# Routed experts: weights stationary with inner units on the partitions, unrolled over 71 tiles, weight-fold products spread over eight tiles

## What is computed

```
logits = x @ Wr / 16                       # 8 experts, top 2 of logits + rb
w      = softmax of the two chosen logits
h      = (x @ W1[e]) * silu(x @ W3[e])     # 256 -> 512
out    = sum of w_e * (h @ W2[e]) over the two chosen e   # 512 -> 256
out   += (x @ Ws1 * silu(x @ Ws3)) @ Ws2   # shared expert
```

## Time and profile before

| | us |
|---|---|
| median of 3 runs | 1294.36 (1294.14 to 1297.22) |
| profiled execution, whole | 1297.05 |
| its span | 1295.3 |
| TensorE busy | 1098.8 (85%) |
| VectorE, ScalarE, GpSimd busy | 843.1, 622.1, 685.3 |
| mean granted clock of TensorE | 0.954 |

### The profile page before, as it was taken

How to read it: one execution, slowest core, us unless ns; L and a number is a source line. 1 busy time by engine, 2 the same in 40 slices (tenths; PEclk the granted TensorE clock), 3 DMA queues, 4 the chain that set the end, 5 groups by cost and what they waited for, 6 DMA issues and landing times. The chain is left out here.

```text
span 1295.3 us, 27552 instructions
## 1 busy us (share of the span) xinstructions
PE 1098.8 (85%) x8532; PEld 829.3 (64%) x8533; DVE 843.1 (65%) x1791; ACT 622.1 (48%) x1483; POOL 685.3 (53%) x794
## 2 busy tenths in 40 slices
PE   4877877888647999799999999997498889699998
PEld 2555555555436787466666656654387777599997
DVE  3999899888747666444444444454588887566664
ACT  3666666666623555233233213322344444566664
POOL 7677677766306766499999566001656650100000
PEclk9999899999868999899999999998699999799999
DMA  1422222222154888735441101112334330111110
GB/s 33 127 91 99 76 100 89 85 85 94 62 191 162 285 274 269 225 136 185 155 154 57 57 25 57 57 53 69 107 115 120 121 106 33 50 50 50 49 49 34
DMA packets 113782, 137.19 MB, mean 106 GB/s; under 512 B 12368, under 2 KB 102448, under 8 KB 111920
## 3 DMA queue, kind: packets, MB, share of 16 engines
q1 hardware_dynamic: 104480, 101.63, 24.5%
q0 software_dynamic: 9232, 34.67, 7.8%
HBM read 83.83 MB, written 52.43 MB: 105 GB/s over the span
## 5 line engine op out<-in xcount | busy, mean ns | idle before, releaser
L253 POOL TENSOR_TENSOR bd<-T,hmask 128x1024 f32<-128x1024 f32 x64 | 150.5, 2372 | 6.9 <-ACT T L371 6.9
L360 ACT ACTIVATE pr<-S,nmx 128x128 f32<-128x128 f32 x512 | 139.3, 396 | 3.9 <-DVE nmx L284 3.9
L956 ACT CAST hT<-HT 128x512 f16<-128x512 f32 x72 | 42.1, 585 | 198.7 <-PE HT L914 198.7
L411 PE MATMUL S<-bd,T 128*128 128x512 f32 x256 | 126.4, 618 | 0.0
L893 PE MATMUL YB<-wm,hT 128*128 x864 | 106.5, 273 | 3.6 <-DVE hT L979 3.6
L893 PE MATMUL Ge<-wm,xT 128*128 x432 | 107.6, 386 | 1.0 <-DVE xT L984 1.0
L893 PE MATMUL Ue<-wm,xT 128*128 x432 | 105.7, 381 | 0.0
L893 PEld LDWEIGHTS YB<-wm,hT 128*128 128x128 f16 x864 | 84.4, 98 | 29.3 <-issue 4.5
L290 DVE SCALAR_TENSOR_TENSOR pT<-PT,pT 128x1024 f16<-128x1024 f32 x64 | 77.6, 1213 | 35.8 <-ACT pT L352 34.6
L1729 PE MATMUL H<-T6s,wm 128*128 128x256 f16 x768 | 96.5, 277 | 1.2 <-DVE T6s L1668 1.2
L1194 POOL DMA_INDIRECT yg<-ys_d,slot x64 | 66.0, 1032 | 58.3 <-POOLq L858 41.2
(11 more groups left out here) (248 smaller groups left out, 2571.1 us busy)
## 6 DMA issues: line engine op xcount, KB each, us to landing
stage<-in_L_ffn_W_dram SPq DMA_DIRECT2D x24, 512.0 KB, 6.1
xs_d<-zeros SPq DMA_DIRECT2D x36, 256.0 KB, 2.4
xe<-xs_d SPq DMA_DIRECT2D x72, 128.0 KB, 2.1
ys_d<-ye SPq DMA_DIRECT2D x72, 128.0 KB, 1.7
bw<-in_L_ffn_up_weights_dram POOLq DMA_DIRECT2D x7, 1024.0 KB, 5.8
bw<-_L_ffn_down_weights_dram POOLq DMA_DIRECT2D x7, 1024.0 KB, 5.6
xb<-in_x_dram SPq DMA_DIRECT2D x32, 128.0 KB, 2.1
cb<-in_ctx_dram SPq DMA_DIRECT2D x32, 128.0 KB, 2.2
```

What stands on the lines that cost most here:

```text
L253: nc.gpsimd.tensor_tensor(out=bd[:, a, c, :, :], in0=T0[:, a, C + c:C + c + 1, :].broadcast_to([P, HH, P]), in1=hmask[:, :, :], op=ALU.mul ...
L360: last = nc.scalar.activation(pr[:, h, i, :], S[h][:, i, :], ACT.Exp, bias=nmx[:, h, i:i + 1])
L411: last = nc.tensor.matmul(S[h][:, i:i + 4, :], T0[:, k % 2, h, :], bd[:, k % 2, h, i:i + 4, :], start=True, stop=True)
```

## The change

The routed stage is rewritten in four points.

- The first two products of an expert are turned round. A 128 by 128 slice of the weights is stationary and the 128 rows of `xT` move, so `Ge` and `Ue` come out with the expert's inner units on the partitions (four blocks `b` of 128 units, `hidden`). 24 products of 128 columns take the place of six of 512, and `hf4` is what `Ye` wants as its stationary side: the transposes of `he` and the bank `HT` are gone. ScalarE rounds `hf4` to the HI part, VectorE subtracts for the LO part, both now from SBUF. `Ye` is as before.
- The tiles are unrolled on all engines; there is no hardware loop in the stage.
- There are `NE` = 71 tiles, not 72.
- The fold's products come two a tile in tiles 48 to 55, into one bank of their own, the eight bias products in tile 47. VectorE copies them in the same tiles and takes the maximum of `wdn` at the end of tile 55, that of `wut` at the end of tile 64. GpSimd goes on after nine of the copies instead of all 17.

The core of the diff:

```diff
+    NE = (NB * TOPK * P + E * (P - 1)) // P
...
-            Ue = [ph.enter_context(nc.psum_tensor(f"Ue{i}", [P, H], F32)) for i in range(2)]
-            Ge = [ph.enter_context(nc.psum_tensor(f"Ge{i}", [P, H], F32)) for i in range(2)]
-            XB = ph.enter_context(nc.psum_tensor("XB", [P, 4, P], F32))
-            HT = ph.enter_context(nc.psum_tensor("HT", [P, HC, P], F32))
-            YB = [ph.enter_context(nc.psum_tensor(f"YB{i}", [P, 2, D], F32)) for i in range(2)]
-            XT, Ye = XB[:, 0:C, :], [y[:, 0, :] for y in YB]
-            Wf, Bf = [y[:, 1, :] for y in YB], XB[:, C, 0:FC]
+            Ue = [ph.enter_context(nc.psum_tensor(f"Ue{i}", [P, HC, P], F32)) for i in range(2)]
+            Ge = [ph.enter_context(nc.psum_tensor(f"Ge{i}", [P, HC, P], F32)) for i in range(2)]
+            XT = ph.enter_context(nc.psum_tensor("XT", [P, C, P], F32))
+            Ye = [ph.enter_context(nc.psum_tensor(f"Ye{i}", [P, D], F32)) for i in range(2)]
+            WB = ph.enter_context(nc.psum_tensor("WB", [P, 2, D], F32))
+            Wf, Bf = WB[:, 0, :], WB[:, 1, 0:FC]
...
-            LATE = 64
-            MID = 44
+            MID, LATE = 47, 64
...
-                    def product(bank, left, kind, e, chunks, width):
-
-                        for i, (xp, wp) in enumerate(PARTS):
-                            for c in range(chunks):
-                                last = nc.tensor.matmul(bank, left[:, xp, c, :],
-                                                        wm[:, kind, bass.ds(e, 1), wp, c * width:(c + 1) * width],
-                                                        start=i == 0 and c == 0, stop=i == 2 and c == chunks - 1)
+                    def hidden(bank, t, kind, e):
+
+                        for b in range(HC):
+                            for i, (wp, xp) in enumerate(PARTS):
+                                for c in range(C):
+                                    last = nc.tensor.matmul(
+                                        bank[:, b, :],
+                                        wm[:, kind, bass.ds(e, 1), wp, c * H + b * P:c * H + (b + 1) * P].rearrange(
+                                            "p o n -> p (o n)"),
+                                        xT[:, t % 2, xp, c, :], start=i == 0 and c == 0, stop=i == 2 and c == C - 1)
                         return last
 
-                    def body(t, k):
-                        if isinstance(t, int) and t < 0:
-                            if t == -1:
-                                xtr(0, 0)
-                            return
-                        a, b = k % 2, (k - 1) % 2
-                        before = experts.get(k - 1)
-                        if before is None and on4(t - 1):
-                            before = expert(t - 1)
-                        experts.clear()
-                        e = experts[k] = expert(t) if on4(t) else None
-                        if on4(t - 1):
-                            pe.wait_ge(s_he, t)
-                            if due(t - 1):
-                                pe.wait_ge(s_hTe, t - 1)
-                            for c in range(HC):
-                                last = nc.tensor.transpose(HT[:, c, :], he[:, b, c * P:(c + 1) * P], ident[:, :])
-                            last.then_inc(s_hT, 1)
-                        if on4(t):
+                    def fold(i):
+                        if i:
+                            pe.wait_ge(s_bv, i + i // FC)
+                        b, w = i % FC, (wut, wdn)[i // FC]
+                        nc.tensor.matmul(Wf, bdiag[:, i // FC, b * P:(b + 1) * P], w[:, b, 0:D],
+                                         start=True, stop=True).then_inc(s_bm, 1)
+
+                    transpose_rows(0)
+                    before = None
+                    for t in range(NE + 1):
+                        e = pe.value_load(tile_expert[0:1, t:t + 1], min_val=0, max_val=E - 1) if t < NE else None
+                        if t < NE:
                             pe.wait_ge(s_xte, t + 1)
-                            if due(t - 1):
+                            if t >= 2:
                                 pe.wait_ge(s_sl4, t - 1)
-                            product(Ge[a][:, :], xT[:, a, :, :, :], 0, e, C, H).then_inc(s_g, 1)
-                        xtr(t + 1, k + 1)
-                        if on4(t):
-                            if due(t - 1):
+                            hidden(Ge[t % 2], t, 0, e).then_inc(s_g, 1)
+                        if t == MID:
+                            pe.wait_ge(s_bo, FOLD_AT)
+                            for b in range(FC):
+                                nc.tensor.matmul(Bf[:, b:b + 1], bdiag[:, 0, b * P:(b + 1) * P], wut[:, b, D:D + 1],
+                                                 start=True, stop=True).then_inc(s_bm, 1)
+                        if MID < t <= MID + FC:
+                            fold(2 * (t - MID) - 2)
+                        transpose_rows(t + 1)
+                        if t < NE:
+                            if t >= 2:
                                 pe.wait_ge(s_he, t - 1)
-                            product(Ue[a][:, :], xT[:, a, :, :, :], 1, e, C, H).then_inc(s_u, 1)
-                        if on4(t - 1):
-                            pe.wait_ge(s_hTe, t)
-                            if due(t - 2):
+                            hidden(Ue[t % 2], t, 1, e).then_inc(s_u, 1)
+                        if MID < t <= MID + FC:
+                            fold(2 * (t - MID) - 1)
+                        if t >= 1:
+                            pe.wait_ge(s_hl4, t)
+                            if t >= 3:
                                 pe.wait_ge(s_yc, t - 2)
-                            product(Ye[b], hT[:, b, :, :, :], 2, before, HC, D).then_inc(s_ye, 1)
-
-                    steps(pe, RANGE4[0], MID, RANGE4[2], MID, 4, body)
-
-                    pe.wait_ge(s_bo, FOLD_AT)
-                    pe.wait_ge(s_xte, MID + 1)
-                    pe.wait_ge(s_yc, MID - 1)
-                    for b in range(FC):
-                        nc.tensor.matmul(Bf[:, b:b + 1], bdiag[:, 0, b * P:(b + 1) * P], wut[:, b, D:D + 1],
-                                         start=True, stop=True).then_inc(s_bm, 1)
-                    for i in range(2 * FC):
-                        b, w = i % FC, (wut, wdn)[i // FC]
-                        if i >= 2:
-                            pe.wait_ge(s_bv, i - 1)
-                        nc.tensor.matmul(Wf[i % 2], bdiag[:, i // FC, b * P:(b + 1) * P], w[:, b, 0:D],
-                                         start=True, stop=True).then_inc(s_bm, 1)
-                    pe.wait_ge(s_bv, 2 * FC + 1)
-                    steps(pe, MID, RANGE4[1], MID, RANGE4[3], 4, body)
+                            for i, (hp_, wp) in enumerate(PARTS):
+                                for b in range(HC):
+                                    last = nc.tensor.matmul(Ye[(t - 1) % 2][:, :], hh4[:, (t - 1) % 2, hp_, b, :],
+                                                            wm[:, 2, bass.ds(before, 1), wp, b * D:(b + 1) * D],
+                                                            start=i == 0 and b == 0, stop=i == 2 and b == HC - 1)
+                            last.then_inc(s_ye, 1)
...
+                        if t >= 0:
+                            act.wait_ge(s_he, t + 1)
+                            if t >= 2:
+                                act.wait_ge(s_ye, t - 1)
+                            nc.scalar.copy(hh4[:, t % 2, HI, :, :], hf4[:, t % 2, :, :]).then_inc(s_hh4, 1)
...
+                    def folded(i):
+                        b, w = i % FC, (wut, wdn)[i // FC]
+                        dve.wait_ge(s_bm, FC + i + 1)
+                        nc.vector.tensor_copy(w[:, b, 0:D], Wf).then_inc(s_bv, 1)
+
+                    def folded_bias():
+                        dve.wait_ge(s_bm, FC)
+                        nc.vector.tensor_copy(wut[:, :, D], Bf).then_inc(s_bv, 1)
+
+                    def largest(i, w):
+                        dve.wait_ge(s_bv, 2 * FC + 1)
+                        nc.vector.tensor_reduce(wmax[:, i:i + 1], w[:, :, 0:D], AX.XY, ALU.max,
+                                                apply_absolute_value=True).then_inc(s_bv, 1)
+
+                    for t in range(-1, NE + 1):
+                        if MID < t <= MID + FC:
+                            folded(2 * (t - MID) - 2)
...
+                        if MID < t <= MID + FC:
+                            folded(2 * (t - MID) - 1)
+                        if t == MID + FC // 2:
+                            folded_bias()
+                        if 0 <= t < NE:
+                            dve.wait_ge(s_hh4, t + 1)
+                            nc.vector.tensor_tensor(hh4[:, t % 2, LO, :, :], hf4[:, t % 2, :, :], hh4[:, t % 2, HI, :, :],
+                                                    ALU.subtract).then_inc(s_hl4, 1)
...
-                    steps(dve, RANGE4[0], MID, RANGE4[2], MID, 4, body)
```

(68 more changed lines are left out.)

56 lines of the change are left out of this document (22 added, 34 removed).

## The result

| | before | after |
|---|---|---|
| median, us | 1294.57 (4 runs, 1294.14 to 1297.22) | 1388.67 (4 runs, 1386.06 to 1389.18) |
| span of the profiled execution | 1295.3 | 1387.5 |
| first row transposes of the stage | 531.92 | 532.42 |
| last `ye` of the stage begins | 894.1 | 987.0 |
| the stage between these two | 362.2 | 454.6 |

The ratio is 1.072, 95% interval 1.070 to 1.0741: slower by 94 us. The whole of it is in the routed stage: it grew by 92.4 us, the span by 92.2.

A forecast was written before the change was run, and what follows sets the result against it. TensorE's sequencer becomes the bound at 6.07 us a tile, over the array's 4.19: 71 x 6.07 = 431.0, less 72 x 4.55 = 327.6, 17.5 (fold) and 1.0 (end), gives +84.9 us, forecast 1379, range 1350 to 1440.

The forecast's parts named there:

- The bound before: Routed stage before the change: TensorE's array is the bound, its products and transposes filling the whole 4.55 us of a tile.
- The array's term: TensorE's array in the changed routed stage: 4.19 us a tile, 0.36 less than before, at 0.0555 a 128-column pair.
- the rival of 1440: Routed stage: weight loads with a register's address aren't quick, a pair costs 0.109, array 6.76 us a tile; chance 0.12.
- The count of sums: TensorE's queue in the routed stage: 40 address sums a tile instead of 16, namely `G` 16, `U` 16, `Y` 8.
- The rival in which they don't multiply: Routed stage: column blocks need no new address sums, so the array's 4.19 us a tile decides, 1258 us; chance 0.13.
- C: Rival tested in the experiments: VectorE's LO subtraction, held up by GpSimd, carries a large part; no chance given.
- The price of a sum: TensorE's queue in the routed stage: 0.127 us for each address sum, 5.08 us a tile for 40.
- 0 to 0.15 us a tile: Fetching of unrolled code in the routed stage, priced at this range and taken as 0.
- The value load and the waits: TensorE's queue in the routed stage: 0.65 us a tile for loading the expert's number, 0.34 for three waits.
- Nothing late there: Other engines in the routed stage: VectorE's steps take 2.1 us of a 6.07 us tile, ScalarE less; none late.
- Fold, clock, tail: Fold hidden in eight tiles gains 17.5 us; stage clock stays 1.00 (falling clock's chance 0.04); shorter last tile gains 1.0.

The follow-up runs named there:

- Experiment 4: Old 512-column products with transposes of `he` kept, but unrolled, 71 tiles and the fold spread, against the kernel before: 1279.3 us, ratio 0.986.
- experiment 1: Changed kernel with each tile's expert fixed when the program is written, so no register addresses; routing's choice left out: 1269.8 us, ratio 0.980 to before.
- experiment 9: The kernel of experiment 8 with the joined sums of `G` and `U` as four, twelve products, four, twelve products: 1249.2 us, ratio 0.963 to before.
- experiment 7: Changed kernel with experts fixed when written (routing's choice left out) and `hf4` kept in PSUM: 1254.8 us, ratio 0.968 to before.
- experiment 8: The kernel of experiment 6 without the two instructions that test the expert's number against 0 and 7: 1255.7 us, ratio 0.969 to before.
- experiment 10: Changed kernel with TensorE's tiles 4 to 43 and 56 to 67 in hardware loops of four, other engines unrolled: 1407.7 us, ratio 1.086 to before.
- experiment 5: Changed kernel with `hf4` kept in PSUM, written over `Ue`, so the subtraction has one SBUF input: 1383.8 us, ratio 1.067 to before.
- experiment 3: Changed kernel with address sums of `G`, `U` and `Y` joined by twos ahead of their products, 20 instructions a tile, not 40: 1285.0 us, ratio 0.992 to before.
- experiment 6: The joined sums of experiment 3 together with `hf4` in PSUM as in experiment 5: 1271.4 us, ratio 0.980 to before.

## Why the prediction held, and where two errors covered each other

Forecast +84.9 us, measured +92.2 in the spans and +94.1 in the medians. Step by step:

- **The bound before.** Right, but the tile was taken from one timeline, 4.55. The mean over 35 is 4.68, since each fourth tile has the turn of the loop, 5.0 us, with idle time put down to issue. 72 x 0.12 = 9 us were missing on the side of before. Experiment 4 shows the 4.56 without the loop.
- **The array's term.** 4.19 forecast, 4.21 measured (experiment 1). A narrow pair 0.0555 forecast, 0.0557 measured; the quick load also works with a register's address, as experiment 9 shows, so the rival of 1440 had no ground.
- **The count of sums.** 32 and 8 a tile, exactly. The rival in which they don't multiply fell with it. Its figure of 1258 for a stage at the array's pace was good all the same: experiments 7 and 8 came to 1255 and 1256, though only with C taken away too.
- **The price of a sum.** Right for looped code: 0.1269 over 390 distances of before, 0.1277 in the loop of experiment 10. Too low for the unrolled kernel: in the late tiles 6.27 us less 0.65 and 0.34 leaves 5.28 for 40 sums, 0.132 each. That is 0.20 us a tile, 71 x 0.20 = 14 us, the largest error. By experiment 10 some 0.16 of the 0.20 come with straight code, the term that the forecast priced at "0 to 0.15 us a tile" and took as 0. It reckoned from six packets and one hitch of a looped kernel, whose queue was not the bound. The value load and the waits: 903.3 - 902.5 = 0.8 with one wait in it, as forecast.
- **"Nothing late there"** for VectorE was wrong. Its 2.1 us took the duration of a subtraction that read a bank for one that reads SBUF twice. It cost 5 to 6 us (experiment 5), and would have cost 14 in a shorter tile (experiments 3 and 6).
- **Fold, clock, tail.** The sixteen products of the fold hide in the tiles: eleven tiles from 815.1 to 884.9 take 6.35 us each, 0.07 over the others (first row below, `ye` in that stretch). The clock was 1.00 in the stretch shown above, as forecast. At the end, from `hf` at 983.18 to the last `Y` at 985.38 are 2.2 us, the number forecast (the timeline behind it).

```profile
L998 DVE TENSOR_SCALAR ye<-Ye x12: 410/416/418, 815.1 to 884.9; 128x256 f32<-128x256 f32 x12
```

```profile
983.18 0.69 DVE L984 SCALAR_TENSOR_TENSOR hf<-Ue,sg 128x512 f32<-128x512 f32 x1 [3.82 <-issue]
...
985.38 1.60 PE L928 MATMUL Ye<-wm,hh 128*128 x12 [0.69 <-DVE hh L992]
```

Together 84.9 + 14 + 6 - 9 = 96 against 92.4 in the stage. The starts of `G` tell most of the remaining 4. In before, tile 64, at which VectorE takes the maxima, lasted 7.3 us, with `Y` 2.1 us idle behind VectorE, and was 2.6 over the mean; the first tile took 6.35, 1.7 over. Neither was in the forecast's 72 x 4.55, and after has no such stop at 64. The first tile of after, which has no `Y`, took 4.9 and was counted with 6.07. That would be 5 to 6 us; the fold's 0.7 goes the other way. The total came out well in part by luck: the mis-sized tiles of before and the mis-sized sums of after have opposite signs.

## What to carry to other kernels

Here an operand whose address hangs on a register cost TensorE's queue one sum for each different slice, and a busy share near 100% doesn't show it: compare the distance of the starts with the width of the products, and count the queue's instructions in a tile. Before cutting wide products into narrow ones, multiply their slices by 0.13 us and set that against the array's time; if it is over, have the sums joined and spread between the products rather than give up the cut. Where the queue is the bound, price unrolling too: straight code took 0.16 us a tile more of it here, though a loop's own work took more still. And when an operand moves from a bank to SBUF, look who else reads SBUF at that time.

## What the runs showed of the hardware that was not expected

- A sum instruction with six operations costs the queue little more than one with three, 0.133 to 0.138 us against 0.124: halving the eight of `Y` gave 0.32 us a tile, and with 20 in place of 40 the tile is 4.2 to 4.6 us instead of 6.27.
- The held-up subtraction lasted up to 6.3 us (median 1.69, smallest 0.72) next to GpSimd products of 1.5 us each; with one input from a bank it was 0.69 every time.
- Eight sums in one block cost time that two blocks of four do not: experiment 9 is 6.5 us under 8 (4.4 in the stage), with the same instructions in another order. A limit on how far the queue can run ahead would explain it; no run measured the limit.
- A packet of instructions on q8 goes with a hitch in the queue: 18 distances of 0.26 to 0.29 us in place of 0.124, each 0.65 to 1.24 us ahead of a packet, and none in a looped stretch without packets.
